# Where the row work, the query low parts and the row transfers stand in a fused attention stage on Trainium2

## The reference

```
h = _L0_tok_ref(...)                       # exp table times x: [32, 128, 1024]
h = concatenate([h, txt], axis=1)          # [32, 205, 1024]
h = h + attention(layernorm(h))            # 32 heads of 32, 8 key/value heads, causal
h = h + ffn(layernorm(h))                  # 1024 x 1024 weight plus low-rank terms, an inverse FFT
```

## Time and profile before

| what | value |
|---|---|
| median of 3 runs | 2897.89 us (2894.68 to 2900.92) |
| the profiled execution | 2894.3 us, its span 2891.9 us |
| busy: TensorE, VectorE, ScalarE, GpSimd | 92%, 67%, 43%, 40% of the span |
| TensorE's mean granted clock | 0.975 |
| first projection of attention | 223.92 us |
| first TensorE work of the tail | 1752.10 us |

### The profile page before, as it was taken

The page is one execution under the profiler, slowest core; times in us unless marked ns, Lnnn a source line. Parts: engine busy times, 40 slices in busy tenths (PEclk is TensorE's granted clock), DMA queues, the critical chain, the costliest instruction groups (busy, mean ns, idle before and its releaser), DMA issues. The chain is left out here.

```text
span 2891.9 us, 70053 instructions
## 1 busy us (share of the span) xinstructions
PE 2655.3 (92%) x27456; PEld 1919.6 (66%) x27456; DVE 1941.2 (67%) x5569; ACT 1230.0 (43%) x2570; POOL 1144.9 (40%) x1810
## 2 busy tenths in 40 slices
PE   1948999999999999999999976999999999999999
PEld 1838888888888888888888952444444444444444
DVE  8966888888888888888888674644444444444443
ACT  4343676766767676766667572201000010101010
POOL 2751565656656565666656570101010101010100
PEclk9979999999999999999999976999999999999999
DMA  7756556465555555565555454454545455545553
GB/s 242 194 122 100 98 92 105 85 109 93 96 94 96 103 93 104 84 107 92 101 92 86 73 124 170 113 139 116 133 122 136 119 134 121 133 123 131 125 129 77
DMA packets 509031, 332.99 MB, mean 115 GB/s; under 512 B 421145, under 2 KB 464409, under 8 KB 508225
## 3 DMA queue, kind: packets, MB, share of 16 engines
q1 hardware_dynamic: 486192, 264.68, 46.3%
q10 hardware_dynamic: 22512, 63.84, 7.1%
HBM read 116.49 MB, written 80.61 MB: 68 GB/s over the span
## 5 line engine op out<-in xcount | busy, mean ns | idle before, releaser
L1044 PE MATMUL psJ<-xth,qh 128*128 128x205 f16 x2048 | 517.3, 253 | 51.6 <-DMA xtl<-xfl 47.6
L704 POOL TENSOR_TENSOR pl<-arena,ph 128x410 f16<-128x410 f32 (+1 forms) x512 | 501.0, 998 | 94.7 <-ACT ph L790 94.7
L1046 PE MATMUL psJ<-xth,ql 128*128 128x205 f16 x2048 | 516.3, 252 | 0.0
L1045 PE MATMUL psJ<-xtl,qh 128*128 128x205 f16 x2048 | 515.8, 252 | 0.0
L699 POOL TENSOR_SCALAR_AFFINE_SELECT arena<-arena 128x256 f32<-128x256 f32 (+1 forms) x768 | 331.7, 438 | 438.3 <-ACT arena L783 419.3
L1261 POOL TENSOR_TENSOR arena<-stage,arena 128x1024 f32<-128x1024 f32 x52 | 122.1, 2349 | 936.2 <-DVE stage L1304 936.2
L1275 ACT CAST xh<-arena 128x1024 f16<-128x1024 f32 x52 | 54.3, 1045 | 995.1 <-DVE arena L1313 995.1
L783 ACT ACTIVATE arena<-psT,escale 128x410 f32<-128x410 f32 (+1 forms) x768 | 399.6, 565 | 95.5 <-PE psT L984 57.5
L790 ACT CAST ph<-arena 128x410 f16<-128x410 f32 (+1 forms) x768 | 334.8, 500 | 14.9 <-POOL arena L699 14.7
L1304 DVE SCALAR_TENSOR_TENSOR stage<-ps5O,osc,h_in 128x512 f32<-128x512 f32 x104 | 77.9, 750 | 388.4 <-PE ps5O L1401 388.4
L885 DVE TENSOR_REDUCE mx<-psS 77x2 f32<-77x410 f32 x512 | 296.5, 579 | 60.7 <-PE psS L1031 57.0
(11 more groups left out here) (231 smaller groups left out, 6106.2 us busy)
## 6 DMA issues: line engine op xcount, KB each, us to landing
a_in<-acat SPq DMA_DIRECT2D x52, 512.0 KB, 3.8
h_in<-hcat SPq DMA_DIRECT2D x52, 512.0 KB, 4.6
qst<-qsh SPq DMA_DIRECT2D x128, 205.0 KB, 4.7
out<-stage SPq DMA_DIRECT2D x51, 512.0 KB, 3.1
hcat<-ob SPq DMA_DIRECT2D x64, 256.0 KB, 4.4
xin<-hcat ACTq DMA_DIRECT2D x32, 512.0 KB
acat<-arena ACTq DMA_DIRECT2D x64, 256.0 KB
qst<-qsl SPq DMA_DIRECT2D x64, 205.0 KB, 5.7
```

The lines of the kernel that those rows point to most:

```text
L704: pool.tensor_tensor(view(pl, g % 2, k), view(p32, g % 2, k), view(ph, g % 2, k), ALU.subtract).then_inc(lo_pool, 1)
L1044: pe.matmul(ps[:, 0:S], wh[:, k, c], xth[:, par, k, 0:S], start=k == 0, stop=False)
L1045: pe.matmul(ps[:, 0:S], wh[:, k, c], xtl[:, par, k, 0:S], start=False, stop=False)
L1046: m = pe.matmul(ps[:, 0:S], wl[:, k, c], xth[:, par, k, 0:S], start=False, stop=k == KC - 1)
```

## The change

- `EXTRA` moves one slot on: values in slots 1 and 2, keys in 3 and 4. Slot 0 has the query unit and one m, slot 4 the query unit, a key unit and the other m.
- ScalarE's `high_part` of element b+3 now runs in the same step as its turn, in slots 1, 2 and 3 (`HIGH`: pieces 0, 1 and 2 with 3), between the copy of the query unit and that of the extra unit; it was done for element b+4 in slots 4 to 7 of the step before. The value copies are split over slots 1 and 2, behind the casts.
- VectorE makes the query unit's low part first wherever the slot has a second unit (`split`), ahead of the rows' low part (`LOW`: slots 2, 3, 4 and 4), of layer-norm (`LINK`: slots 1 to 3) and of the normalising.
- Row loads and stores are issued by SyncE. Its order in a step is now: second restacks, first shift, store, transposes of the image rows (for b of 0 and more; each part has its own wait), first restacks, value transposes, transposes of the text rows, second shift, store, load. For b below 0 all four row transposes stand behind the first restacks.
- Of the tail's loads one small one goes out at the end of each of steps 1 to 13, and wo at the end of step 29.
- `rs` and `nmean` get two buffers. GpSimd's rounds move from slot 3 to slot 4; for the first element VectorE runs them. The rows' low parts of the first element alternate with the weights' low parts. The load of element 1 waits for that of element 0.
- In `ssm` the pieces of the peaks lie two chunks earlier, and the peaks go out one chunk earlier.

```diff
             for ch in range(NCH):
-                if ch == NCH - 1:
+                if ch == NCH - 2:
                     sp.wait_ge(peaks_ok, 1)
                     sp.dma_start(acat[0, 0:2 * P].rearrange("(p t) -> p t", t=2), peaks[:]).then_inc(peaks_out, 16)
+                if ch == NCH - 1:
                     sp.wait_ge(peaks_out, 16)
...
-                if ch >= NCH - 12:
-                    weight_peak(ch - (NCH - 12))
+                if NCH - 14 <= ch < NCH - 2:
+                    weight_peak(ch - (NCH - 14))
...
-        EXTRA = {0: ("v", 0), 1: ("v", 1), 2: ("k", 0), 3: ("k", 1)}
+        EXTRA = {1: ("v", 0), 2: ("v", 1), 3: ("k", 0), 4: ("k", 1)}
+        HIGH, LOW, LINK = {1: (0,), 2: (1,), 3: (2, 3)}, {2: (0,), 3: (1,), 4: (2, 3)}, {1: 0, 2: 1, 3: 2}
+        FIRST_HIGH, FIRST_LOW = {2: (0,), 3: (1,), 4: (2, 3)}, {3: (0,), 4: (1,), 5: (2, 3)}
...
-                if b == B - 2:
-                    for q in v_in:
-                        sp.wait_ge(q, 32 * B)
-                    for dst, src, arrived in ahead:
-                        sp.dma_start(dst, src).then_inc(arrived, 16)
-                if has["turn"]:
+                if has["last"]:
+                    store(b - 1, 1)
+                if has["turn"] and b >= 0:
                     wait(sp, pj_filled, base)
                     turn(0, nxt, b + 3)
-                    turn(1, nxt, b + 3)
...
+                if has["turn"] and b < 0:
+                    wait(sp, pj_filled, base)
+                    turn(0, nxt, b + 3)
+                    turn(1, nxt, b + 3)
+                if has["qkv"]:
+                    wait(sp, pj_lo, base + at(rows, "v", 1) + 1)
                     wait(sp, v_ok, 2 * (b + 2))
...
+                if has["turn"] and b >= 0:
+                    turn(1, nxt, b + 3)
                 if has["max"]:
                     wait(sp, pj_lo, base + at(rows, "m", 0) + 1)
                     shift_rows(0, nxt)
+                if has["att"]:
+                    store(b, 0)
+                if has["load"]:
+                    sp.wait_ge(x_lo, 4 * (b + 4))
+                    load(b + 5, 1 - par)
+                if 1 <= b < len(ahead):
+                    dst, src, arrived = ahead[b]
+                    sp.dma_start(dst, src).then_inc(arrived, 16)
+                if b == B - 3:
+                    for q in v_in:
+                        sp.wait_ge(q, 32 * B)
+                    dst, src, arrived = ahead[0]
+                    sp.dma_start(dst, src).then_inc(arrived, 16)
...
             def turn(t, to, n):
+                sp.wait_ge(x_hi, 4 * n + 2 * t + 2)
+                sp.dma_start_transpose(out=xth[:, to, :, cols], in_=xfh[0:r, t, :]).then_inc(xt_in[t], 16)
                 sp.wait_ge(x_lo, 4 * n + 2 * t + 2)
-                sp.dma_start_transpose(out=xth[:, to, :, cols], in_=xfh[0:r, t, :]).then_inc(xt_in[t], 16)
                 sp.dma_start_transpose(out=xtl[:, to, :, cols], in_=xfl[0:r, t, :]).then_inc(xt_in[t], 16)
+            load(0, 0)
+            sp.wait_ge(x_in[0], 32)
+            load(1, 1)
...
# ScalarE
-                    if g == 3 and has["load"]:
-                        act.wait_ge(x_lo, 4 * (b + 4))
-                        load(b + 5, 1 - par)
-                    if g == 2 and has["last"]:
-                        store(b - 1, 1)
-                    if g == 2 and has["max"]:
-                        values(b + 1)
-                    if g == 6 and has["att"]:
-                        store(b, 0)
...
+                    if g in (1, 2) and has["max"]:
+                        values(b + 1, g - 1)
+                    pieces = (HIGH if b >= 0 else FIRST_HIGH).get(g, ()) if has["turn"] and b > -3 else ()
...
+                        if i == 0:
+                            for piece in pieces:
+                                high_part(b + 3, piece)
-                    if g >= 4 and has["ln"]:
-                        high_part(b, par, g - 4)
...
# VectorE
+                    if b == -4:
+                        rsqrt_rounds(link, dve, rs[:, b % 2])
+                        dve.tensor_scalar(nmean[:, b % 2], mv[:, :, 0], -1.0, None, ALU.mult).then_inc(ln_done, 1)
...
-                    if has["turn"] and g == 0:
-                        low_part(b + 3, 3)
-                    if has["ln"]:
-                        if g in (1, 2, 3):
-                            layer_norm(b, par, g - 1)
-                        if b == -4 and g == 3:
-                            weights_low(0)
-                        for piece in {6: (0,), 7: (1, 2)}.get(g, ()):
-                            low_part(b + 4, piece)
-                        if b == -3 and g == 0:
-                            weights_low(1)
+                    split = 0
+                    if len(rows[g]) > 1 and rows[g][0][0] == "q":
+                        split_unit(b, par, (k0 + n) % 2, *rows[g][0], base + n + 1)
+                        n += 1
+                        split = 1
+                    if b == -3 and g == 0:
+                        for part, ks in (((0, 1), (4, 5)), ((2, 3), (6, 7))):
+                            for piece in part:
+                                low_part(0, piece)
+                            weights_low(0, ks)
+                        weights_low(1, range(KC))
+                    if has["turn"] and b > -3:
+                        for piece in (LOW if b >= 0 else FIRST_LOW).get(g, ()):
+                            low_part(b + 3, piece)
+                    if has["ln"] and g in LINK:
+                        layer_norm(b, par, LINK[g])
+                    if b == -4 and g == NKV - 1:
+                        weights_low(0, range(4))
```

More of the change, by code:

```diff
@@ L626, in step, with load, store @@
                     shift_rows(0, nxt)
+                if has["att"]:
[11 more added lines that the diff above has]
+                    sp.dma_start(dst, src).then_inc(arrived, 16)
+            def load(b, par):
+                sp.dma_start(xin[:, par, 0, :], hcat[b * S:b * S + P, :]).then_inc(x_in[par], 16)
+                sp.dma_start(xin[0:TXT, par, 1, :], hcat[b * S + P:b * S + S, :]).then_inc(x_in[par], 16)
+            def store(b, half):
+                c = slice(half * D // 2, (half + 1) * D // 2)
+                sp.wait_ge(norm_done, 8 * b + 4 * half + 4)
+                sp.dma_start(acat[b * S:b * S + P, c], ao[:, half, 0, :]).then_inc(a_out[half], 16)
+                sp.dma_start(acat[b * S + P:b * S + S, c], ao[0:TXT, half, 1, :]).then_inc(a_out[half], 16)
             def shift_rows(half, to):
@@ L678, in step @@
                 if not has["att"]:
-                    if has["ln"]:
+                    if has["ln"] and b > -4:
                         scale_rows(b)
                     if b == -4:
-                        pool.memset(ph[:], 0.0)
-                        pool.memset(pl[:], 0.0)
+                        pool.memset(ph[:, :, 2, :], 0.0)
+                        pool.memset(pl[:, :, 2, :], 0.0)
                     if b == -3:
@@ L705, in step @@
                                            ALU.subtract).then_inc(lo_pool, 1)
-                    if g == 3 and has["ln"]:
+                    if g == 4 and has["ln"]:
                         scale_rows(b)
@@ L739, in values @@
                 wait(act, av_done, 8 * (n - 1))
-                for k, dst in enumerate((vh, vl)):
-                    v = vt[:, k].rearrange("p t (g d) -> p t g d", d=HD)
-                    act.copy(dst[n % 2][:, :, :, 0:HD], v).then_inc(v_ok, 1)
+                v = vt[:, k].rearrange("p t (g d) -> p t g d", d=HD)
+                act.copy((vh, vl)[k][n % 2][:, :, :, 0:HD], v).then_inc(v_ok, 1)
             def weights_high(n):
@@ L759, in step @@
                 if b == -3:
+                    for n in range(4):
+                        high_part(0, n)
+                    n = 0
                     weights_high(1)
@@ L790, in step @@
                             act.copy(view(ph, g % 2, k), view(p32, g % 2, k)).then_inc(hi_done, 1)
-                    for kind, m in rows[g]:
+                    if g in (1, 2) and has["max"]:
+                        values(b + 1, g - 1)
+                    pieces = (HIGH if b >= 0 else FIRST_HIGH).get(g, ()) if has["turn"] and b > -3 else ()
+                    if not rows[g]:
+                        for piece in pieces:
+                            high_part(b + 3, piece)
+                    for i, (kind, m) in enumerate(rows[g]):
                         src, hi, _ = unit_views(kind, m, (k0 + n) % 2, b, par)
@@ L814, in _, with weights_low @@
             dve.wait_ge(cleared, 1)
-            def weights_low(n):
-                for k in range(KC):
+            def weights_low(n, ks):
+                for k in ks:
                     dve.wait_ge(w_hi, n * KC + k + 1)
@@ L849, in layer_norm @@
                         dve.wait_ge(x_in[par], 32 * ((b + 4) // 2 + 1))
+                        wait(dve, ln_done, b + 4)
                     chain.n = 3 * g
@@ L957, in step @@
```

(2 more changed lines are left out.)

46 lines of the change are left out of this document (18 added, 28 removed).

## The result

| kernel | median | lowest to highest | ratio to before, 95% interval |
|---|---|---|---|
| before, same chip | 2897.38 us (4 runs) | | 1 |
| changed | 2824.48 us (4 runs) | 2819.37 to 2829.54 | 0.9748 [0.9727, 0.9768] |

The account below looks back on a forecast made before the run. TensorE, busy 92% of the span, bounds the kernel, with 3.56 us of stalls a step. 2894.3 - 56 (steady) - 1.8 (steps 28, 29) - 5.5 (start) - 2 (end) = 2829.0, or 2831 against the runs' median; range 2796 to 2888.

Parts of the forecast that it names:

- The account of before: Steady attention step before the change: 46.32 us, of which 42.76 without a stall and 3.56 of TensorE stalls.
- ScalarE: Steady step: DMA issues go and high parts sit behind TensorE's extra unit, so 1.9 us of stalls a step go.
- VectorE: Steady slots 1 to 7 and 0: late low parts and layer-norm leave stalls, chiefly 1.1 us in slot 3.
- Slot 5's 0.3: Steady step: slot 5's q unit waits 0.3 us for the bank of the k split ending late in slot 4.
- SyncE: Steady step: transposes and ml shift land just in time, margin 1.8 to 2.5 us at the medians; cost 0.1 a step.
- The start: Block's start to step 0: TensorE 13 us earlier, step -2 1.7 shorter, less 2.9 and 6.3 of waits; 5.5 us saved.
- The step -2 is 28.9 us: Start: step -2 takes 28.9 us instead of 30.6, as a 2.96 us wait for a low part goes and 1.3 stays.
- The row load has 9 us until layer-norm: Load issued at the step's end has 9 us before layer-norm reads it, more than the 6.9 of the first load.
- The end: Step 30's 4.09 us wait for a shift behind weight loads: 4.2 less 2.2 for the 4 MB load, 2 us saved.
- A: Steady steps: VectorE is the new bound, idle before early q splits in four slots; 0.4 a step saved, 2874; chance 0.15.
- B: Steady steps: everything fits, stalls of 0.5 us a step, 2798 us; chance 0.12.
- C: Each step's first projection: SyncE's last transpose too late, 4.1 us a step, 2941 us (2878 at mid-reach); chance 0.18.

Follow-up runs that it names:

- value-copy run: Changed kernel with both value copies of steps 0 and up ahead of slot 2's exponentials, as before the change: 2813.52 us, ratio 0.9719.
- the best version: Changed kernel with value copies in slot 4, step -1's maxima shift and row loads of steps -2 and -1 ahead of value transposes: 2794.84 us, ratio 0.9647.

## Why the prediction was right, and where it was wrong

**The account of before.** 42.76 us without a stall is borne out to 0.4 us: the period went 46.32, 43.86, 43.37 (values in front), 43.15 (values in slot 4), and in the last slots 0, 3 and 6 are still 0.1 to 0.2 over their plain lengths. No run reached 42.76.

**ScalarE.** Right. The wait in slot 2 and the small ones are gone, and moving the high parts behind both copies alone brought a period of 46.39. That placement is a condition for the whole steady gain.

**VectorE.** Stalls after are 43.86 - 42.76 = 1.1 a step, forecast 1.6. Slot 3 has 0.8 (forecast 1.1, with maxima starting at +1.75 against +2.06: the low part took 0.91 and not 1.1). Slots 6 and 0 have 0.19 and 0.13, for which 0.2 stood. Slot 5's 0.3 didn't come. Over 28 steps this term was 15 us too small. Of the cause of slot 3's stall the prediction put the weight on the low part: it saw the query copy pushed to s+4.4 but counted it as given, while the value-copy run shows that taking this push away removes the stall, as taking the low part out of slot 2 does. Of the early split it saw only the cost; it is worth 28 us.

**SyncE.** The conclusion held, its numbers were too kind. Over steps 1 to 27 the last row transpose went out at s4+13.6 to 15.1 (forecast 13.6) and the ml shift at s4+15.5 to 17.3 (forecast 15.6; 17.1 in the step shown). From its issue to its reader the shift had 2.1 to 3.9 us, with a median landing of 1.9. The slip is in the issue times, by 0.9 us at the median and 1.7 at most. With a shorter period it starts to show: with the value copies in slot 4 there are 3 waits for the shift, 3.0 us in all, in 1200 us, and 2 of 3.1 us in the best version.

**The start.** This sub-step failed, in sign: forecast -5.5, measured 291.47 - 286.76 = +4.7. The first projection (-14.5 against -13), row 1's transposes (3.17 against 2.9) and the shift (5.82 against 6.3) were right. "The step -2 is 28.9 us" was wrong: without its last wait it took 32.7, with waits of 0.85 and 1.99 us for VectorE's low parts and a clock of 0.90. And step -1 took 40.35 us instead of 32.26: SyncE's order was followed for the shift but not for the row load. "The row load has 9 us until layer-norm" was worked out for the steady step only.

**The end.** -1.6 for -2; a wait of 3.42 us for a shift stays at 1624.75, with wo issued at 1604.97 ahead of it. Whether wo causes it wasn't tried.

**Why the total fitted.** By luck in part. Steady steps 15.0 and steps 28 and 29 1.6 better; start 10.2, end 0.4 and tail 1.7 worse; the profiled time lay 1.8 above its span and not 2.4. 2829.0 - 16.6 + 12.3 - 0.6 = 2824.1. Two errors of 10 to 15 us cancelled. (The tail's 1.7 is no more than its spread: the rest took 1178 to 1184 us in the kept traces, with the same instructions.)

**The rivals.** A (VectorE the bound, 0.4 a step less) didn't happen. B (stalls of 0.5) is what the value copies in slot 4 reach, at 0.4. C didn't happen: no wait for a row transpose stands at a steady step's first projection, in the changed kernel or any run. What SyncE's order can cost showed at another place, the shift that step's first scores wait for: 109 and 124 us with a bulk transfer beside it. There the wait alone, which is how C was priced, understates the cost: 47 of 108 us were the clock's.

**Open.** Which of the restacks and transposes near it made the mid-step shift land later (4.2 us for 1.9) wasn't isolated; nor whether ScalarE's store alone made the shift late where ScalarE issued the transfers, and why that cost some 14 us more than SyncE with the load ahead.

## What to carry to other kernels

Work that fills an engine's slack belongs where that engine waits for its producer anyway, between two dependent copies; the same instructions one place later cost all that had been won, and a 0.5 us copy ahead of what another engine waits for cost 15 us. The small transfer that is read next goes ahead of bulk ones, and an order on one engine's queue doesn't protect it from bulk that another engine issues. And a queue's order that is right in the steady step has to be walked through again for each step of the start, load by load.

## What the runs showed of the hardware

- A small shift (6.4 KB) took 1.9 us to land (median of the last one of each step), but 4.2 us with a row load issued just ahead of it by the same engine, and 4.8 us in the run where ScalarE issued loads and stores, with its store moving beside the shift.
- The granted clock: in the kernel before, after 47.64 us of idle, 4.3 us at 0.50; in the changed kernel, after a single wait of 4.31 us in a busy stretch, 5.4 us at 0.50 again. That wait cost over half as much again as it lasted (2.7 us behind 4.31). A wait of 1.2 to 4.2 us in each step, as with the load ahead of the shift, brought the clock down 24 times in 27 steps; the few waits of up to 1.5 us of the run with the values in slot 4 never did.
- GpSimd's operations on 128x2 elements took 1.10 to 1.26 us each beside VectorE's 1024-wide low parts, and 0.19 to 0.20 from 199.67 on, when these had ended (199.54), with no change in the operation: four slow and eight fast. In the kernel before, VectorE's low parts ran from 196.26 to 205.92, and eight were slow (1.10 to 1.29) and four fast.
